# One chunk loop of a graph kernel on one core: the low parts of the split edges as one VectorE operation, behind the six next one-hots

## The reference

```python
in_agg  = segment_sum(edge_feat, receivers, 6250)      # 200000 edges x 64, receivers sorted
out_agg = segment_sum(edge_feat, senders, 6250)        # the same edges, senders in no order
h = relu(concat([in_agg, out_agg, x], 1) @ W1 + b1)    # 192 -> 256
x = layernorm(x + h @ W2 + b2)                         # 256 -> 64
```

## Time and profile before

| what | value |
|---|---|
| median of 3 runs | 1481.49 us (1477.98 to 1488.18) |
| profiled execution, own time | 1473.92 us |
| its span, first to last instruction | 1472.1 us |
| mean granted TensorE clock | 0.967 of full |
| busy: PE, PEld, DVE | 1190.2, 976.6, 1213.3 us |
| busy: ACT, POOL | 991.9, 1104.0 us |

### The profile page before, as it was taken

The page is one execution under the profiler, slowest core; times in us unless marked ns, Lnnn a source line. Parts: engine busy times, 40 slices in busy tenths (PEclk is TensorE's granted clock), DMA queues, the critical chain, the costliest instruction groups (busy, mean ns, idle before and its releaser), DMA issues.

```text
span 1472.1 us, 63779 instructions
## 1 busy us (share of the span) xinstructions
PE 1190.2 (81%) x23123; PEld 976.6 (66%) x23123; DVE 1213.3 (82%) x3787; ACT 991.9 (67%) x2259; POOL 1104.0 (75%) x663
## 2 busy tenths in 40 slices
PE   3667678877888888888888888898888889898896
PEld 2646477767777777777777766666666666666743
DVE  6665788888888988889888888888888888888776
ACT  6334588878888888888888865566556556565432
POOL 3878777867688888877888788877776787777533
PEclk9976899999999999999999989999999999999998
DMA  9332599989899999999999988888878888887641
GB/s 294 31 40 17 90 195 197 195 182 195 174 208 202 195 202 207 196 192 200 210 236 226 218 207 204 186 191 190 206 177 195 202 200 193 201 189 168 151 133 59
DMA packets 262841, 263.21 MB, mean 179 GB/s; under 512 B 106099, under 2 KB 223956, under 8 KB 262486
## 3 DMA queue, kind: packets, MB, share of 16 engines
q1 hardware_dynamic: 170152, 231.66, 54.4%
q0 software_dynamic: 92384, 28.77, 26.2%
q10 hardware_dynamic: 144, 0.52, 0.1%
HBM read 146.90 MB, written 113.96 MB: 177 GB/s over the span
## 4 chain that ended last, share of the span: by engine, by line
PE 67%; issue 12%; ACT 8%; DVE 7%; DMA 2%; ACTq 1%; SPq 1%; DVEq 0%; another core or an unknown queue 0%; POOL 0%
PE psum L1677 24%; PE psum L1701 23%; PE psum L1653 6%; ACT slots_out L864 3%; PE psum L1755 2%; PE psum L1660 2%; DVE to_node L1324 2%; PE psum L1888 1%; PE psum L1616 1%; DMA feat<-in_edge_attr 1%; PE psum L1753 1%; PE psum L1843 1%; ACT again_sign L882 1%; DVE same L1351 1%; ACT parts L843 1%
## 5 line engine op out<-in xcount | busy, mean ns | idle before, releaser
L769 POOL DMA_INDIRECT out_tables<-payload,target x628 | 1070.6, 1705 | 297.5 <-issue 166.1
L1677 PE MATMUL psum<-parts,to_slot 128*128 128x194 bf16 x4836 | 476.5, 250 | 123.1 <-ACT slots_out L864 80.7
L1677 PEld LDWEIGHTS psum<-parts,to_slot 128*128 128x128 bf16 x4836 | 404.7, 98 | 166.3 <-ACT slots_out L864 97.1
L864 ACT ACTIVATE slots_out<-psum 128x388 bf16<-128x388 f32 x936 | 386.2, 473 | 104.2 <-PE psum L1677 78.3
L1701 PE MATMUL psum<-to_node,slots_in 64*64 64x286 bf16 x10296 | 391.2, 285 | 60.7 <-issue 51.6
L1701 PEld LDWEIGHTS psum<-to_node,slots_in 64*64 64x64 bf16 x10296 | 306.6, 106 | 133.4 <-issue 119.9
L1285 DVE TENSOR_SCALAR to_slot<-iota_h,slot 128x528 bf16<-128x528 f16 (+1 forms) x936 | 302.5, 371 | 59.8 <-PE psum L1677 38.2
L1324 DVE TENSOR_SCALAR to_node<-iota_h,slot_rel 128x286 bf16<-128x286 f16 x858 | 247.4, 309 | 20.2 <-PE psum L1701 19.5
L939 ACT ACTIVATE to_node<-apart 128x286 bf16<-128x286 bf16 x286 | 118.0, 436 | 114.6 <-PE psum L1701 113.4
L1324 DVE TENSOR_SCALAR to_node<-iota_rows,slot_rel 128x286 bf16<-128x286 f16 x572 | 194.4, 340 | 0.0
L1239 DVE TENSOR_TENSOR rest<-feat,parts 128x512 f32<-128x512 f32 (+1 forms) x176 | 131.1, 745 | 24.1 <-ACT parts L843 15.5
(11 more groups left out here) (138 smaller groups left out, 909.3 us busy)
## 6 DMA issues: line engine op xcount, KB each, us to landing
slot_tiles<-slots_out SPq DMA_DIRECT2D x156, 388.0 KB
feat<-in_edge_attr SPq DMA_DIRECT2D x195, 256.0 KB
slots_in<-slot_tiles SPq DMA_DIRECT2D x168, 242.5 KB
slots_in<-slot_tiles SPq DMA_DIRECT2D x168, 230.4 KB
slot_tiles<-slots_out SPq DMA_DIRECT2D x78, 291.0 KB
out_tables<-payload,target POOLq DMA_INDIRECT x628
out_tables<-zeros POOLq DMA_DIRECT2D x4, 1600.0 KB
feat<-out_tables SPq DMA_DIRECT2D x48, 128.0 KB, 2.3
```

What stands on the lines that cost most here:

```text
L769: e.indirect_dma_start(out_tab, at, payload[b][:, t, :], None, element_offset=k * TABLE_ROWS * D, compute_op=ALU.add).then_inc(s_tab[k], 16)
L864: e.activation(slots_out[b][:, g:g + n, m, :], ps_share[r % BANKS][:, 0:n * SLOT_W].rearrange("p (g w) -> p g w", w=SLOT_W), ACT.Copy).the ...
L1677: last = e.matmul(ps_share[r % BANKS][:, o:o + SLOT_W], to_slot[m][:, COLUMN_FROM[k] + t * P:COLUMN_FROM[k] + (t + 1) * P], parts[b][:, SH ...
```

## The change

In each sharing chunk on VectorE, `split_lo` for the next chunk is one operation over all 16 columns in place of two over eight. It no longer stands after four of the six next one-hots, with the second window sum between its halves; all six one-hots come first, then the second window sum, then the low parts. Nothing else moves; the rests stay in halves.

```diff
                 to_slots(s, 1, (5,))
                 if not no_more:
-                    to_slots(s + 1, 0, (0, 1, 2, 3))
-                split_lo(c + 1, 1 - b, (0,))
+                    to_slots(s + 1, 0, range(MINI))
                 add_window(c, b, ats, 1)
-                split_lo(c + 1, 1 - b, (1,))
-                if not no_more:
-                    to_slots(s + 1, 0, (4, 5))
+                split_lo(c + 1, 1 - b)
```

## The result

| | median us | lowest to highest | runs |
|---|---|---|---|
| kernel before | 1484.77 | 1466.08 to 1490.88 | 20 |
| kernel after | 1492.83 | 1481.85 to 1501.88 | 20 |

The ratio is 1.0101 with an interval of [1.0072, 1.0131], but it leaves out runs of the kernel before that were counted as disturbed; over all 20 runs of each kernel the medians stand 1492.83 / 1484.77 = 1.0054 apart, 8 us, and the means 1.0060 [1.0037, 1.0083]. So the change makes the kernel slower, by 0.5 to 1 per cent. The profiled execution after took 1495.92 us, span 1494.1 us, at a granted clock of 0.972. The forecast was 1480 us and no difference; 1492.83 us lies inside the range of 1466 to 1497 us, so what failed is "no difference" and not the range.

The account below looks back on a forecast made before the run. The prediction took a ring of waits between PE and ACT's evictions as the bound. A 1 us gain took the profiled 1473.9 to about 1473 us; with that execution 7.6 us below the median, it forecast 1480 us, range 1466 to 1497.

Parts of the forecast that it names:

- The ring: Sharing loop: PE's slot matmuls and ACT's evictions wait for each other, setting 8.88 us per chunk; DVE is idle 1.18 us.
- The sum of the part by part: DVE's merged low parts: 2.10 us becomes 1.92, at most 14.0 us over the loop; 1 us taken as gain.
- The order: DVE's reordered one-hots, window sum and low parts: r0's slack grows from 0.3 to 0.5 us, giving about nothing.
- Cost nothing: Second window sum starts at about 706.85 instead of 706.90; PE reads its semaphore 6 us later, so no cost.
- The faster rival: DVE is in the ring in quick chunks, so 0.18 us returns every chunk: 14 us, 1467.5 us; chance 0.15.
- The slower rival: Six one-hots in a row hold up POOL's scatters by up to 0.66 us: 27 us lost, 1508 us; chance 0.14.

Follow-up runs that it names:

- order alone: Kernel before with six one-hots and second window sum ahead of the low parts, still two operations: 0.9996 to 1.0018 on quick chips, 1.0057 on a slow one.
- merging alone: Kernel before with the low parts as one operation where the first half stood: 1.0027, 0.9997 and 1.001, all on quick chips.
- no scatter: Kernel after without the four scatters of each sharing chunk: 0.9937, 0.9942 and 0.9947 of before, all on quick chips.
- the third call: Slow chip: kernel before profiled again (1493.53 us); kernel after with an extra VectorE operation ahead of the low parts, 1462.92 us; kernel after with targets early, 1444.35 us.

## Why the prediction was wrong

*The ring.* Held. PE's waits for evictions stayed near 70 us, the pace of the 74 chunks is 8.97 us after and 8.90 before, inside the 0.1 us that the prediction allowed, and on a quick chip the change measured 1.0004. That sign of being right was too coarse: 0.07 us over 78 chunks is 5 us.

*The sum of the part by part.* The low part was sized right, 1.21 us, and from the fourth one-hot to `same` DVE took 1.96 us in the median, against 1.9. The later low parts cost nothing, as costed: 0.60 us more ahead of them did not slow the kernel. DVE's busy time did not fall by 12 us; it rose from 1213.3 to 1224.3, with the one-hots at 385 ns in place of 371 (before 302.5 us in all, after 310.8). Part of that is no effect of the change, since the second profile of before has 1222.2 us and 377 ns. But the prediction's remark that a scatter stretches the one-hots, by 0.1 to 0.3 us on DVE, was right: on quick chips the one-hots took 375 to 377 ns in the mean with order alone, 364 to 366 ns with merging alone and 359 to 360 ns with no scatter, and DVE was busy for 1203 to 1206 us with order alone and 1188 to 1189 us with merging alone.

*The failed step.* It is the term of *The order*, "Cost nothing", with the sentence behind it, "The rests, `target` and the scatters' issue are not passed by anything". The prediction looked for somebody who waits for what the change makes earlier or later, found nobody, and set the cost of the order at nothing. Order alone measured 1.0057 [1.0011, 1.0103] on a slow chip, 8 to 10 us, and 0.9996 to 1.0018 in five measurements on quick ones. The prediction named the way out in its last sentence, a phase "set by DVE's order after all", and gave it no mechanism and no price. What the runs show in its place is a phase between GpSimd and PE: on a slow chip GpSimd waits for `target` in many chunks (58 times in 74 chunks after and 36 with order alone, 23 and 50 in the two profiles of before), and a scatter that has waited begins where its pause hits the window sums. In the execution of after a held-up chunk took 9.09 us and any other 8.45. Two things stay open: how the order of VectorE brings GpSimd into that wait, for the kernel before falls into it too; and how much of the loss it is, for the pauses of after are largely made up elsewhere. In the third call, kernels with 7 and 4 held-up chunks took 32 and 46 us less for the 74 chunks than after, and 27 and 41 us less than before, so most of what these two kernels win was to be had before the change.

*The faster rival.* It did not come, and had its reason wrong: 0.60 us more of VectorE work a chunk slowed nothing on a slow chip, and on quick chips neither part measured under 0.999.

*The slower rival.* The sign was right and the mechanism was not. It had longer one-hot runs hold scatters up, with a mean above 1.78 us; the mean was 1.61 us in the stretch. The Trainium skill, "SBUF — State Buffer", section "Who interferes with whom", has VectorE in a two-port mode and GpSimd block each other for the whole of an instruction. That a run of six would so lengthen a scatter is what the prediction made of it, and this trace does not bear it out: a scatter that began 0.09 us behind the first of six one-hots took 1.55 us, and one of the six took 0.65 us where the others took 0.34 to 0.42. Why some scatters grow to 2.70 us stays unexplained.

*What stays open.* Why an execution enters and leaves the state; what part of the 8 us falls behind the sharing chunks, where the kernel before alone took 611.7 us in one execution and 631.4 us in another; whether merging alone costs anything on a slow chip.

## What to carry to other kernels

An engine with slack still has a phase. Where some instruction disturbs another engine at a fixed distance behind its start, ask what releases it: an engine that waits starts at a fixed place in every turn, and if that place is a bad one every turn meets the disturbance; an engine that is behind drifts over it. Then ask what the disturbance costs, for a pause ahead of a wait can be free. Try a change of order on more than one chip before calling it neutral: the same diff measured 1.0004 on one and 1.0101 (1.0060 over all runs) on another. And take a second profile of the kernel before: here its two profiles differ as much as before and after do.

## What the runs showed of the hardware

- Chips differ by 7 to 8% on this kernel at the same granted clock, 0.97: before took 1372 to 1376 us on four chips and 1476 to 1485 us in three calls, two of them known to be different chips.
- On the slow ones PE stands still for 0.4 to 0.6 us with nothing in the profile to wait for, 168 times in six profiles of 74 chunks; 161 of these pauses end 1.15 to 1.45 us behind the start of an indirect DMA on GpSimd. In eleven profiles on quick chips there is not one.
- Indirect DMAs stretch VectorE's one-hots on both kinds of chip: of 936 one-hots 74 took over 0.55 us after on a slow chip, 44 on a quick one, and 1 without the scatters of the sharing chunks; undisturbed they take about 0.35 us. By order the number on quick chips is 43 to 48 with six next one-hots in a row and 6 to 11 with four and two.
- On the quick ones taking all the sharing chunks' scatters away gains 0.6%.
